# Low words of a graph network's weights: a third of them moved from GpSimd to VectorE, and two root products in three terms

## What is computed

```python
def _rgcn_conv(x, weight, root, bias, src, dst, etype):
    out = x @ root + bias                     # 768 x 768
    for r in range(NUM_REL):                  # 3 in layers 0 and 1, 4 in layers 2 to 4
        ...
        h_r = x @ weight[r]                   # 768 x 768
        msgs = h_r[src] * norm[:, None]       # 1 / (edges of this relation into dst)
        out = out + jax.ops.segment_sum(msgs, dst, num_segments=n)
    return out
```

## Time and profile before

| what | value |
|---|---|
| median of 3 runs | 884.61 us (883.16 to 885.83) |
| the profiled execution, its own time | 885.03 us |
| its span, first to last instruction | 883.2 us |
| busy: TensorE / VectorE / GpSimd / ScalarE | 91% / 68% / 59% / 43% |
| mean granted TensorE clock | 0.974 of full speed |

### The profile page before, as it was taken

One profiled execution on the slowest core, in us unless ns is written; L12 is line 12 of the kernel. 1 busy time (PEld: TensorE's weight loads), 2 busy tenths in 40 slices (PEclk: granted clock), 3 DMA queues, 4 the chain that ended last, 5 costly groups with the idle time before them and its releaser, 6 DMA issues.

```text
span 883.2 us, 10141 instructions
## 1 busy us (share of the span) xinstructions
PE 802.7 (91%) x4034; PEld 632.6 (72%) x4034; DVE 601.9 (68%) x675; ACT 383.1 (43%) x434; POOL 517.7 (59%) x225
## 2 busy tenths in 40 slices
PE   8999999999878999988988769999999998887987
PEld 4569976776645799666655449997997898764674
DVE  8965158999997521989999967535852899254451
ACT  1124356667553343767755524432432342142521
POOL 0346629999996472899999926661873378000000
PEclk9999999999899999999999989999999999979999
DMA  9036516344332452440533238532752653500000
GB/s 366 2 92 230 170 45 166 74 136 151 102 113 72 155 172 102 132 107 1 203 107 109 71 108 286 192 130 100 252 183 74 227 203 108 220 30 1 1 1 36
DMA packets 24262, 110.98 MB, mean 126 GB/s; under 512 B 3604, under 2 KB 5908, under 8 KB 23832
## 3 DMA queue, kind: packets, MB, share of 16 engines
q1 hardware_dynamic: 23096, 104.24, 36.2%
q10 hardware_dynamic: 1120, 6.10, 1.8%
HBM read 100.63 MB, written 0.79 MB: 115 GB/s over the span
## 4 chain that ended last, share of the span: by engine, by line
PE 56%; POOL 28%; DVE 11%; ACT 3%; issue 1%; DMA 0%; DVEq 0%; ACTq 0%
PE ps L941 22%; POOL prod L542 18%; PE ps L889 9%; POOL prod L545 6%; PE ps L926 6%; DVE prod L1649 5%; POOL w_lo L530 4%; PE ps L1313 3%; PE ps L996 2%; PE ps L1017 2%; PE ps L1372 2%; PE ps L1174 1%; DVE qi_t L1667 1%; PE ps L1298 1%; PE ps L895 1%
## 5 line engine op out<-in xcount | busy, mean ns | idle before, releaser
L530 POOL TENSOR_TENSOR w_lo<-w_raw,w_hi 128x1536 fp32r<-128x1536 f32 x54 | 201.1, 3735 | 145.3 <-ACT w_hi L596 145.1
L542 POOL TENSOR_TENSOR prod<-prod 128x1024 f32<-128x1024 f32 x94 | 226.4, 2424 | 42.4 <-DVE prod L1649 42.2
L701 ACT ACTIVATE prod<-ps 128x1024 f32<-128x1024 f32 x192 | 187.8, 1024 | 98.2 <-PE ps L1127 75.9
L1649 DVE TENSOR_TENSOR prod<-prod,ps 128x2048 f32<-128x2048 f32 x96 | 218.6, 2278 | 3.2 <-ACT prod L701 2.5
L1127 PE MATMUL ps<-sel_pair,h_and_q 128*128 128x512 f32 x384 | 130.7, 453 | 20.9 <-ACT prod L701 20.7
L889 PE MATMUL ps<-w_raw,h_t 128*128 128x384 f32 x408 | 141.9, 495 | 0.0
L596 ACT ACTIVATE w_hi<-w_raw 128x1536 fp32r<-128x1536 f32 x54 | 80.3, 1488 | 136.6 <-PE ps L941 93.2
L941 PE MATMUL ps<-w_hi,yt_hi 128*128 128x384 f32 x432 | 111.6, 339 | 8.1 <-POOL w_lo L530 8.1
L889 PEld LDWEIGHTS ps<-w_raw,h_t 128*128 128x128 f32 x408 | 78.6, 194 | 46.0 <-issue 2.6
L941 PE MATMUL ps<-w_lo,yt_hi 128*128 128x384 f32 x432 | 110.4, 336 | 0.0
L941 PE MATMUL ps<-w_hi,yt_lo 128*128 128x384 f32 x432 | 110.3, 336 | 0.0
(11 more groups left out here) (182 smaller groups left out, 992.2 us busy)
## 6 DMA issues: line engine op xcount, KB each, us to landing
w_raw<-weights SPq DMA_DIRECT2D x105, 768.0 KB, 4.4
wa_in<-weights SPq DMA_DIRECT2D x6, 768.0 KB, 5.9
w_gat<-weights SPq DMA_DIRECT2D x6, 768.0 KB, 8.2
w_query<-weights SPq DMA_DIRECT2D x3, 768.0 KB, 11.4
h_and_q<-stage_hi SPq DMA_DIRECT2D x24, 96.0 KB, 2.1
h_and_q<-stage_lo SPq DMA_DIRECT2D x24, 96.0 KB, 2.2
a_vec<-gat_vectors ACTq DMA_DIRECT2D x1, 2048.0 KB, 8.1
q_t<-queries ACTq DMA_DIRECT2D x1, 1536.0 KB, 10.5
```

Source lines behind the costliest of these rows:

```text
L530: pool.tensor_tensor(Wl[:, j, :], raw_slab(U, 0, j), Wh[:, j, :], ALU.subtract).then_inc(w_lo_ready, 1)
L542: pool.tensor_tensor(v[:, :, 0:32], v[:, :, 0:32], v[:, :, 32:64], ALU.add).then_inc(folded_once, 1)
L701: act.activation(slot_view(s)[:, :, 32 * u:32 * u + 32], args.rearrange("p b (n l) -> p (b n) l", l=LH), ACT.Sigmoid).then_inc(sigmoid_rea ...
L1649: TT(slot_view(s), slot_view(s), ps[:, 6, o:o + L].unsqueeze(1).broadcast_to([P, NB, L]), ALU.mult).then_inc(products_ready, 1)
```

## The change

1. VectorE takes the low pass of slab 2 of every relation (`w_lo(U, 2)`, in its list ahead of the next relation's `relation`, and ahead of the counts of layer 4), and of all three slabs of the roots of layers 3 and 4. GpSimd keeps slabs 0 and 1 of the relations. The semaphore `w_lo_ready` becomes two.
2. The roots of layers 3 and 4 are products in three terms (`root_part`, `three_terms`), with their features split into `yt_hi` and `yt_lo` (`root_hi` on ScalarE, `root_lo` on VectorE) instead of copied into `h_t`. Both tiles' roots now stand ahead of aggregation 1.
3. At the end of layer 4 `logit_weights(0, ...)` stands ahead of the low pass of relation 4's slab 2.

```diff
-SPLIT = [UNIT[l] + v + 1 for l in range(LAYERS) for v in range(RELATIONS[l])]
+SPLIT = [UNIT[l] + v for l in range(LAYERS) for v in range(l < 3, RELATIONS[l] + 1)]
+ROOTS = [UNIT[l] for l in range(3, LAYERS)]
...
+LO_BY_VECTOR = [(u, 0, j) for u in SPLIT for j in range(3) if u in ROOTS or j == 2]
+LO_BY_POOL = [(u, 0, j) for u in SPLIT for j in range(2) if u not in ROOTS]
...
@@ GpSimd
-            def w_lo(U, js=(0, 1, 2)):
-
-                for j in js:
+            def w_lo(U):
+
+                for j in range(2):
                     pool.wait_ge(w_hi_ready, SPLIT_AT[U, 0, j])
...
@@ ScalarE
+            def root_hi(layer, t):
+
+                act.wait_ge(turned[t], layer + 1 if t == 0 else INPUT[layer] + 1)
+                copy(YTh[:, 0, :, t * P:(t + 1) * P], chunk_tile(4 + 2 * t, KC)).then_inc(root_hi_ready[t], 1)
...
                     relu_out(layer, 0)
-                    keep_turned(layer + 3, layer + 2)
+                    w_hi(UNIT[layer + 1], (0,))
+                    root_hi(layer + 1, 0)
+                    h_hi(layer + 1, 0)
+                    w_hi(UNIT[layer + 1], (1,))
+                    relu_out(layer, 1)
+                    w_hi(UNIT[layer + 1], (2,))
+                    h_hi(layer + 1, 1)
+                    root_hi(layer + 1, 1)
                     w_hi(UNIT[layer + 1] + 1, (0,))
-                    h_hi(layer + 1, 0)
-                    relu_out(layer, 1)
-                    h_hi(layer + 1, 1)
...
@@ TensorE
+            def root_part(layer, t, j):
+
+                if j == 0:
+                    pe.wait_ge(root_lo_ready[t], layer - 2)
+                    root_bias(layer, pair(layer, t))
+                wait_lo(pe, UNIT[layer], j)
+                mm = three_terms(0, j, t, pair(layer, t), False)
+                if t == 1:
+                    mm.then_inc(w_used, 1)
...
                 if layer > 2:
-                    root(layer, 0, 0, 4)
-                turn(1, e)
-                root(layer, 0, 4, KC)
+                    root_part(layer, 0, 0)
+                    turn(1, e)
+                    root_part(layer, 0, 1)
+                    root_part(layer, 0, 2)
+                else:
+                    turn(1, e)
+                    root(layer, 0, 4, KC)
...
+                if layer > 2:
+                    for j in range(3):
+                        root_part(layer, 1, j)
...
                 aggregate(layer, 1)
-                root(layer, 1, 4 if degrees is not None else 0, KC)
+                if layer < 3:
+                    root(layer, 1, 4 if degrees is not None else 0, KC)
                 aggregate(layer, 2)
...
@@ VectorE
+            def root_lo(layer, t):
+
+                dve.wait_ge(root_hi_ready[t], layer - 2)
+                cols = slice(t * P, (t + 1) * P)
+                TT(YTl[:, 0, :, cols], chunk_tile(4 + 2 * t, KC), YTh[:, 0, :, cols], ALU.subtract).then_inc(root_lo_ready[t], 1)
+
+            def w_lo(U, j):
+
+                dve.wait_ge(w_hi_ready, SPLIT_AT[U, 0, j])
+                TT(Wl[:, j, :], raw_slab(U, 0, j), Wh[:, j, :], ALU.subtract).then_inc(w_lo_by_vector, 1)
...
                 for v in range(1, RELATIONS[i] + 1):
+                    if v > 1:
+                        w_lo(UNIT[i] + v - 1, 2)
                     relation(i, v)
+                w_lo(UNIT[i] + RELATIONS[i], 2)
...
                 if layer > 2:
+                    w_lo(UNIT[layer], 0)
+                    root_lo(layer, 0)
                     h_lo(layer, 0)
-                    keep_turned(layer + 2)
+                    w_lo(UNIT[layer], 1)
+                    w_lo(UNIT[layer], 2)
+                    root_lo(layer, 1)
                     h_lo(layer, 1)
                 for v in range(1, RELATIONS[layer] + 1):
+                    if v > 1:
+                        w_lo(UNIT[layer] + v - 1, 2)
...
+                if layer == LAYERS - 1:
+                    wait_landed(dve, 30, 0, 0)
+                    logit_weights(0, raw_slab(30, 0, 0), 0, 6, True)
+                w_lo(UNIT[layer] + RELATIONS[layer], 2)
```

More of the change, by code:

```diff
@@ L264, in build @@
         turn_kept = [sem(f"turn_kept{t}") for t in range(NT)]
+        root_hi_ready = [sem(f"root_hi_ready{t}") for t in range(NT)]
+        root_lo_ready = [sem(f"root_lo_ready{t}") for t in range(NT)]
         half_turned = sem("half_turned")
@@ L933, in product @@
                 U = UNIT[layer] + v
[L934 to L935 removed]
+                wait_lo(pe, U, j)
                 pe.wait_ge(yt_lo_ready, BEFORE[layer] + 3 * (v - 1) + (j + 1))
[L937 to L943 removed]
+                return three_terms(v % 2, j, t, pair(layer, t), last)
             def layer_products(layer, degrees=None):
```

47 lines of the change are left out of this document (24 added, 23 removed).

## The result

The changed kernel takes 908.12 us (median of 4 runs, 905.6 to 909.96), the kernel before 883.88 on the same chip: ratio 1.0268, interval 1.0246 to 1.0289. It is 24.2 us slower. The profiled execution took 905.6 us (span 903.8).

A forecast was written before the change was run, and what follows sets the result against it. TensorE, busy 91% of the span, was taken as the bound. Terms 0.4 + 0.7 + 4.2 + 3.5 + 12.3 + 3 x 1.8 = 26.5 on the profiled 885.03 gave 911.5, so 911.0 us for the median; range 889 to 924.

The forecast's parts named there:

- the likeliest case: Whole kernel: slower, 911.0 us for the median, own range 899 to 921; chance 0.71.
- 2.2 us saved, twice: Gaps ahead of layers 3 and 4: three-term roots cut turn's start to first product from 27.4 to 25.2 us.
- The rival that the root saves nothing in its gap: Gaps ahead of layers 3 and 4: root's low words come late, no 2.2 terms, 915 us; chance inside the 0.71.
- The walk: Layers 0 to 4: slab-by-slab times of ready low words against TensorE's due times, giving +0.4, +0.7, +4.2, +3.5, +12.3 us.
- Layer 2: Relations 3 and 4: late slabs and logit work make TensorE wait, layer end 600.25 against 596.05, +4.2 us.
- The point I named as deciding: Layer 2, relation 4: whether logit work ends before (4,2)'s high words at 584.1; forecast 589.25, 5.1 us too late.
- Layer 3: Relations 2 to 4: slabs wait 5.7 us more than now; less the 2.2 from the start, +3.5.
- Layer 4: Counts and logit products delay relations 2 to 4: waits of 20.5 us, less 6.1 now and 2.2 saved, +12.3.
- The clock: Layers 2 to 4: after long waits TensorE runs at the lower 1.2 GHz level, losing 1.8 us each.
- Only layer 4 suffers: Layers 2 and 3 absorb the lateness, layer 4 has 14.5 + 1.8 more waits: 898 us, or 891; chance 0.12.
- the faster case: Whole kernel: the slab fits VectorE's idle time, waits of layers 0 to 3 go, 875 us; chance 0.12.
- The wash: Whole kernel: layer 4's waits grow just by the starts' 4.4, rest hidden, 882 to 887 us; chance 0.05.

The follow-up runs named there:

- roots-only run: Changed kernel with every relation's low passes back on GpSimd, keeping only the three-term roots of layers 3 and 4: 890.81 us, 1.0061 of the kernel before.
- The slabs alone: Kernel before with only slab 2 of each relation moved to VectorE, in the changed kernel's places, roots staying plain fp32: 914.59 us, ratio 1.0327.
- the run with the last slab first: Changed kernel with the low pass of relation 4's slab 2 ahead of relation 4's logit weights in layers 2 and 3 only: 897.49 us, ratio 1.0139.

## Why the prediction was right, and where it was not

911.0 was forecast and 908.12 measured, inside the range and with the likeliest case. By its steps (forecast, then stretch against stretch):

- Layers 0 and 1: +0.4 and +0.7; measured +0.28 and +0.56. Right.
- "2.2 us saved, twice": measured 2.08 twice, and again in the roots-only run. The rival that the root saves nothing in its gap is refuted. Its work "fits", as forecast: the first product of layer 3 comes 25.15 us after the turn's start (592.44 to 617.59), for 25.2. What failed is that the root was counted as a saving alone. With GpSimd making all low words it costs 9.9 in layer 4 behind the gap. The walk saw that aggregation 1 comes late to the first product, and charged the result to the slabs; the price of counts under a GpSimd slab (9.5 instead of the 3.15 of the earlier trace rows) was nowhere in it. In the changed kernel they ran unblocked, at 3.16 (the blocked instruction was the low pass ahead of them, 3.80). The slabs alone cost 14.4 there and both together 15.8, so the sum came out right though the cause was only half named.
- Layer 2: +4.2 and 1.8 for the clock; measured +5.23. The last slab, predicted to be waited for 3.15, was waited for 2.96, and the next twelve matmuls took 3.76 (586.44 to 590.20) instead of 2.09. The point I named as deciding, the end of the logit work 5.1 us after the high words (4.7 measured, 584.45 after 579.71), was the right one: the run with the last slab first moved just this and gave 6.0 back.
- Layer 3: +5.7 and 1.8 behind the gap; measured +6.56.
- Layer 4: 14.5 and 1.8; measured 15.79. Waits at relation 4 of 5.6, 2.9 and 6.6 were forecast; 5.30, 0.72 and 6.51 came. (At relations 2 and 3: 3.0, 0.9, 0.6 and 0.8 forecast; 2.54, 0.51, 0.53 and none came.) The 0.72 is smaller than forecast because TensorE reached it late: the first slab ran at the low clock and took 4.21 (4.93 less 0.72). So the clock's loss took most of the wait behind it (-2.2), and in layer 4 it fell twice (the last slab's first matmuls took 4.01), which I had counted once (+2.2). The two errors cancel, which is luck. Relation 4 ends 29.6 us after its predecessor, for "nearly 30".
- The clock: I put 1.8 in each of layers 2 to 4. Layer 2's 1.7 is measured, and in layer 3 the twelve matmuls behind the same wait took 3.60, 1.5 over 2.09. The window above, 0.58 from 586 to 590, is the twin of the earlier trace rows: the lower level of 1.2 GHz for most of it, after a wait of 2.96 us. In the terms of the Trainium skill, "TensorE: Matmul & The Clock Gate", section "What's actually happening", an idle array falls to half rate; this run agrees, with the 0.84 us that a pair of matmuls takes from 587.14 on, 0.51 once the clock is back.
- Waits for low words were put at some 35 us and were 27.7. The middle wait of layer 4 is 2.2 of the difference. Another part is how a wait is counted: behind a wait of 0.48, relation 3 of layer 2 took 13.43, 0.78 over its usual 12.65, so a wait costs TensorE some 0.3 more than its row shows, and there are 16. The rest are waits that were smaller than forecast.
- The rivals. "Only layer 4 suffers" is refuted by layers 2 and 3; the faster case needed three layers in a row to clear, and none did. The same work with the pass one place later in the list does clear them (41.2, 56.7 and 57.2 in layers 1 to 3), but that is another kernel. The wash fell with these two.

## What to carry to other kernels

When work moves from a loaded engine to one with idle time, the slot in the receiver's list counts, not its idle share: put the moved instruction behind what releases other engines, and ahead of work that nothing waits for yet, above all of work that itself waits for a load. Look at each stage for itself: in layer 4 the place behind made slab (1,2) late by 3.99. Take each part of a change alone before believing where its gain is, since a part that shortens one gap shifts everything behind it, here constant tables and edge counts, under another engine's work. Where two engines exclude each other, build constants in a stretch in which the other is idle.
